# A new order of the first stage, and the second attention's blend in fp32r parts

## The reference

```python
weight = softmax(einsum('bct,bcs->bts', q * s, k * s))      # first attention, 512 x 512, over channels
h = einsum('bts,bcs->bct', weight, v)                        # 125 x 512
# second attention on layernorm(h): 8 heads of 64, 2 key/value heads, rope
scores = tanh((q2 @ k2.T) / 16 / 50) * 50
h = h + (softmax(scores) @ v2) @ Wo.T
# feed-forward on y = layernorm(h): a shared part for every token ...
out = (silu(y @ sw1) * (y @ sw3)) @ sw2
# ... and two of eight experts per token, by softmax(y @ gate_w) + expert_bias
out = out.at[token_idx].add(routed_out)
h = h + out
```

## Time and profile before

| | us |
|---|---|
| median of 3 runs | 5918.14 |
| the profiled execution's own time | 5922.86 |
| its span, first to last instruction | 5921.1 |
| TensorE busy, share of the span | 5784.0, 98% |
| VectorE busy | 4450.0, 75% |
| ScalarE busy | 3084.8, 52% |
| GpSimd busy | 2101.8, 35% |

### The profile page before, as it was taken

How to read it: one execution, slowest core, us unless ns; L and a number is a source line. 1 busy time by engine, 2 the same in 40 slices (tenths; PEclk the granted TensorE clock), 3 DMA queues, 4 the chain that set the end, 5 groups by cost and what they waited for, 6 DMA issues and landing times. The chain is left out here.

```text
span 5921.1 us, 109291 instructions
## 1 busy us (share of the span) xinstructions
PE 5784.0 (98%) x32259; PEld 5009.4 (85%) x32259; DVE 4450.0 (75%) x10104; ACT 3084.8 (52%) x5748; POOL 2101.8 (35%) x1711
## 2 busy tenths in 40 slices
PE   5999999999999999999999997899999999999999
PEld 4888888888888888888888886899999999999998
DVE  4888888888888888888888886666666766666665
ACT  3555555555555555555555553555555555555554
POOL 1333333333333333333333332333434444444343
PEclk8999999999999999999999999999999999999999
DMA  2111111111111111111111111777777777777762
GB/s 73 47 50 44 44 49 46 43 47 49 43 45 50 44 44 49 46 43 47 49 43 45 50 44 25 190 188 187 184 189 182 182 187 188 183 189 182 184 167 79
DMA packets 363663, 565.45 MB, mean 95 GB/s; under 512 B 92898, under 2 KB 187106, under 8 KB 363492
## 3 DMA queue, kind: packets, MB, share of 16 engines
q1 hardware_dynamic: 294276, 433.22, 24.2%
q0 software_dynamic: 69344, 131.70, 11.3%
HBM read 438.14 MB, written 138.42 MB: 97 GB/s over the span
## 5 line engine op out<-in xcount | busy, mean ns | idle before, releaser
L1438 POOL DMA_INDIRECT out_dram<-res,goal x273 | 560.8, 2054 | 1070.4 <-DMA entries<-routed_entries 480.8
L930 POOL TENSOR_SCALAR ve<-ag 125x1 f32<-125x1 f32 x256 | 56.1, 219 | 1618.3 <-DVE ag L755 942.2
L639 ACT ACTIVATE e<-ps,negmax 128x512 f32<-128x512 f32 x512 | 348.6, 685 | 513.5 <-PE ps L449 409.8
L1188 PE MATMUL ps<-rT_hi,up_hi 128*128 128x384 f32 x2548 | 552.3, 338 | 1.6 <-DVE rT_lo L1348 1.6
L1188 PE MATMUL ps<-rT_lo,up_hi 128*128 128x384 f32 x2548 | 552.1, 338 | 0.0
L1188 PE MATMUL ps<-rT_hi,up_lo 128*128 128x384 f32 x2548 | 552.0, 338 | 0.0
L1278 ACT ACTIVATE uT_hi<-egb 128x384 fp32r<-128x384 f32 x364 | 191.4, 526 | 572.3 <-DVE egb L1367 561.5
L1188 PEld LDWEIGHTS ps<-rT_hi,up_hi 128*128 128x128 f32 x2548 | 457.8, 188 | 9.8 <-issue 2.0
L1188 PEld LDWEIGHTS ps<-rT_lo,up_hi 128*128 128x128 f32 x2548 | 456.3, 188 | 0.0
L1188 PEld LDWEIGHTS ps<-rT_hi,up_lo 128*128 128x128 f32 x2548 | 456.2, 188 | 0.0
L942 POOL TENSOR_TENSOR qk_low<-X,qk_high 125x1024 fp32r<-125x1024 f32 x128 | 306.3, 2393 | 345.7 <-ACT qk_high L626 345.7
(11 more groups left out here) (220 smaller groups left out, 15549.2 us busy)
## 6 DMA issues: line engine op xcount, KB each, us to landing
raw<-in_L_ffn_w SPq DMA_DIRECT2D x182, 768.0 KB, 5.1
X<-in_x SPq DMA_DIRECT2D x128, 750.0 KB
raw<-in_L_ffn_w SPq DMA_DIRECT2D x91, 896.0 KB
raw<-in_L_ffn_w SPq DMA_DIRECT2D x273, 128.0 KB, 5.0
normed_rows<-y SPq DMA_DIRECT2D x128, 250.0 KB
out_dram<-h SPq DMA_DIRECT2D x128, 250.0 KB
rows<-normed_rows,entries POOLq DMA_INDIRECT x273
out_dram<-res,goal POOLq DMA_INDIRECT x273
```

The source lines that it names most:

```text
L639: nc.scalar.activation(e[:, i, :], ps[:, (i + 1) % 2, :], ACT.Exp, bias=negmax[:, i:i + 1], accum_out=total[:, i:i + 1]).then_inc(e_sb.sem, 1)
L1188: ins = nc.tensor.matmul(ps[:, bank, 0:GROUP], w[a][:, k, col:col + P], rT[b][:, k, :], start=(k == 0 and i == 0), stop=(k == KC - 1 and i ...
L1438: nc.gpsimd.indirect_dma_start(out, bass.IndirectOffsetOnAxis(ap=goal[group[1] % 2][:, i:i + 1], axis=0), res[i][:], None, bounds_check=la ...
```

## The change: what it does, and the diff

1. `attend` is done in fp32r parts. ScalarE rounds prob to `prob_cut[0]` (`soften_hi`), GpSimd makes `prob_cut[1] = prob - prob_cut[0]` (125 x 1000) . `vS` holds, per key/value head, the high values (64), a one, a zero, and the low values (64), so that one product of prob's high part with 130 columns gives both; prob's low part is multiplied by 66 columns. The fourth head of a bank has no room for 130 columns and uses 66 + 64 + 66. It makes 18 fp32r products per batch in place of 8 fp32 ones. `normalise` now adds the two halves: per key/value head two reciprocals, a multiply of 125 x 192, a multiply of 125 x 64, and three scalar_tensor_tensor of 125 x 64.
2. `attend` and `normalise` move one step later (lag 2), and so the shared feed-forward's second half (w3s, gate, choice, transposes of gb, down, ranks, placed) moves to lag 3. w1g of batch f is the last work of TensorE's step.
3. The normalising of e moves from VectorE to ScalarE (four Copies with a scale).
4. All five queues get a new order. On GpSimd it is: rstd 1, prob's low part, v's low part, the rope's add, rstd 2, the next q and k's low part, and the scatter last. On SyncE's queue the two output DMAs swap places.

The order of TensorE's step after: scores 0, 1 (t); w3s (g); scores 2, 3; transposes of v (t); of xn (a); `attend(0)`, `attend(1)` (f); q (a); transposes of gb (g); of attn (f); e 0, 1 (t); k/v (a); wo (f); e 2, 3 (t); down, all 11 (g); ranks (g); rope's transposes (a); blend high (t); transposes of y (f); second scores (a); blend low (t); w1g (f).

```diff
@@ TensorE @@
                     def attend(kv):
-                        pe.wait_ge(qkT_lo.sem, qkT_lo.at(a))
-                        pe.wait_ge(p_sb.sem, p_sb.at(a, kv + 1))
                         for j in range(G):
-                            last = nc.tensor.matmul(ps[0:C, 2 + kv, j * VW:(j + 1) * VW],
-                                                    prob[0:C, kv, j * C:(j + 1) * C],
-                                                    vaug[a[1] % 2][0:C, kv, :], start=True, stop=True)
+                            heads = slice(j * C, (j + 1) * C)
+                            wide = 2 * HD + 2 if j < APART else EW
+                            col = j * (2 * HD + 2)
+                            nc.tensor.matmul(ps[0:C, 7 - kv, col:col + wide], prob_cut[0][0:C, kv, heads],
+                                             vS[0:C, kv, 0:wide], start=True, stop=False)
+                            if j >= APART:
+                                nc.tensor.matmul(ps[0:C, 7 - kv, col:col + HD], prob_cut[0][0:C, kv, heads],
+                                                 vS[0:C, kv, EW:EW + HD], start=False, stop=False)
+                            last = nc.tensor.matmul(ps[0:C, 7 - kv, col:col + EW], prob_cut[1][0:C, kv, heads],
+                                                    vS[0:C, kv, 0:EW], start=False, stop=True)
                         last.then_inc(pv_ps.sem, 1)
...
+                    if has(2):
+                        pe.wait_ge(p_hi.sem, p_hi.at(f))
+                        pe.wait_ge(p_lo.sem, p_lo.at(f))
+                        pe.wait_ge(v_lo.sem, v_lo.at(f))
+                        pe.wait_ge(gb_sb.sem, gb_sb.at(g))
+                        attend(0)
+                        pe.wait_ge(ga_sb.sem, ga_sb.at(g))
+                        attend(1)
...
+                    if has(2):
+                        pe.wait_ge(attn_sb.sem, attn_sb.at(f))
+                        pe.wait_ge(xT_lo.sem, xT_lo.at(a))
+                        turn(3, attn[:, :, :].rearrange("p a b -> p (a b)")).then_inc(aT_ps.sem, 1)
@@ ScalarE @@
+                        for i in range(KC):
+                            nc.scalar.activation(e[:, i, :], e[:, i, :], ACT.Copy,
+                                                 scale=rz[:, i:i + 1]).then_inc(e_norm.sem, 1)
...
+                    def soften_hi(kv):
+                        act.wait_ge(p_sb.sem, p_sb.at(a, kv + 1))
+                        act.wait_ge(pv_ps.sem, pv_ps.at(f))
+                        nc.scalar.activation(prob_cut[0][0:C, kv, :], prob[0:C, kv, :], ACT.Copy).then_inc(p_hi.sem, 1)
@@ VectorE: order of the step after: bn 1 (a), nl (g), maxima 0, xn (a), ga, gb (g), maxima 1, chosen, m16 (g), xT_lo (a),
@@ 1/total (t), normalise 0, 1 (f), aT_lo (f), hT_lo (g), v_lo (a), e_lo 0, 1 (t), rope (a), h2, bn 2 (f), e_lo 2, 3 (t), y (f),
@@ h3 (g), qkT_lo (a), entries (g), yT_lo (f), placed (g)
+                    def normalise(kv):
+                        dve.wait_ge(pv_ps.sem, pv_ps.at(f, kv + 1))
...
+                        nc.vector.reciprocal(rd_v[:, 0:APART], both[:, :, HD])
+                        nc.vector.reciprocal(rd_v[:, APART:G],
+                                             flat[:, APART * wide + HD:APART * wide + HD + 1]).then_inc(rden_sb.sem, 1)
...
+                        nc.vector.tensor_tensor(ours[:, 0:APART, :], both[:, :, EW:wide],
+                                                rd_v[:, 0:APART, None].to_broadcast([C, APART, HD]),
+                                                ALU.mult).then_inc(both_sb.sem, 1)
+                        nc.vector.tensor_scalar(ours[:, APART, :], flat[:, APART * wide:APART * wide + HD],
+                                                rd_v[:, APART:G], None, ALU.mult)
+                        dve.wait_ge(both_sb.sem, both_sb.at(f, kv + 1))
+                        for j in range(APART):
+                            last = nc.vector.scalar_tensor_tensor(ours[:, j, :], both[:, j, 0:HD], rd_v[:, j:j + 1],
+                                                                  ours[:, j, :], ALU.mult, ALU.add)
+                        last.then_inc(attn_sb.sem, 1)
@@ GpSimd @@
                     if has(1):
                         rstd(a, ag1, ve1, rs1, ag1_sb, ve1_sb, rs1_sb, xn_sb)
                     if has(2):
+                        pool.wait_ge(p_hi.sem, p_hi.at(f))
+                        pool.wait_ge(pv_ps.sem, pv_ps.at(g))
+                        alone(pool)
+                        nc.gpsimd.tensor_tensor(out=prob_cut[1][0:C, :, :], in0=prob[0:C, :, :],
+                                                in1=prob_cut[0][0:C, :, :].bitcast(F32),
+                                                op=ALU.subtract).then_inc(p_lo.sem, 1)
...
                         rstd(f, ag2, ve2, rs2, ag2_sb, ve2_sb, rs2_sb, y_sb)
+                    if has(-1):
+                        cut_scores(back(t, -1))
                     if has(3):
                         pool.wait_ge(pick.sem, pick.at(g))
                         pool.wait_ge(place.sem, place.at(g))
```

More of the change, by code:

```diff
@@ L343, in alone, with product @@
             eng.sem_inc(past, 1)
-        def product(pe, dst, lhs, rhs, rows, c0, c1, lo, at, between=None):
+        def product(pe, dst, lhs, rhs, rows, c0, c1, lo, at):
             for i, (a, b) in enumerate(PASSES):
                 if i == 2:
-                    if between:
-                        between()
                     pe.wait_ge(lo, at)
@@ L397, in step @@
                         load(back(t, -1))
[L398 to L402, removed]
                     if has(2):
@@ L480, in step @@
                         scores(1)
-                    if has(2):
-                        pe.wait_ge(attn_sb.sem, attn_sb.at(f))
+                    if has(3):
                         pe.wait_ge(tanh_sb.sem, tanh_sb.at(f))
[L485 to L488, removed]
+                        product(pe, ps[0:C, 7, 0:HID], yT, w3s, P, 0, HID, yT_lo.sem, yT_lo.at(g)).then_inc(up_ps.sem, 1)
+                    if has(0):
+                        scores(2)
+                        scores(3)
                     if has(0):
                         pe.wait_ge(x_in.of(t), x_in.at(t))
-                        pe.wait_ge(attn_sb.sem, attn_sb.at(f))
+                        pe.wait_ge(qkT_lo.sem, qkT_lo.at(f))
                         for k in range(KC):
@@ L496, in step @@
                         last.then_inc(vT_ps.sem, 1)
-                    if has(3):
-                        down_part(2, 1)
-                        pe.wait_ge(hT_lo.sem, hT_lo.at(g))
-                        down_part(0, 0, c=1)
-                    if has(0):
-                        scores(2)
-                    if has(0):
-                        scores(3)
+                    if has(1):
+                        pe.wait_ge(xn_sb.sem, xn_sb.at(a))
+                        pe.wait_ge(place.sem, place.at(back(g, 1)))
+                        turn(3, xn).then_inc(xT_ps.sem, 1)
@@ new lines, in step @@
+                    if has(2):
[6 more added lines that the diff above has]
+                        attend(1)
+                    if has(1):
+                        pe.wait_ge(yT_lo.sem, yT_lo.at(g))
+                        pe.wait_ge(xT_hi.sem, xT_hi.at(a))
+                        product(pe, ps[0:C, 4, :], xT, wqkv, P, 0, D, xT_lo.sem, xT_lo.at(a)).then_inc(q_ps.sem, 1)
@@ L508, in step @@
                         product(pe, ps[0:C, 7, :], aT, woT, P, 0, D, aT_lo.sem, aT_lo.at(f)).then_inc(wo_ps.sem, 1)
[L509 to L539, removed]
-                        pe.wait_ge(h3_sb.sem, h3_sb.at(g))
-                        product(pe, ps[0:C, 6, 0:HG], yT, w1g, P, 0, HG, yT_lo.sem, yT_lo.at(f)).then_inc(up_ps.sem, 1)
                     if has(0):
@@ L692, in step @@
                         weights_hi(3)
-                    if has(-1):
-                        round_scores(back(t, -1))
                     if has(1):
@@ L792, in step @@
                     if has(1):
                         dve.wait_ge(xT_hi.sem, xT_hi.at(a))
[L794 to L800 removed]
+                        lo_part(xT, 3).then_inc(xT_lo.sem, 1)
@@ L974, in step @@
                         alone(pool)
-                        nc.gpsimd.tensor_tensor(out=qkr[0:C, :], in0=rc[0:C, :], in1=rsn[0:C, :],
+                        nc.gpsimd.tensor_tensor(out=rc[0:C, :], in0=rc[0:C, :], in1=rsn[0:C, :],
                                                 op=ALU.add).then_inc(rope_add.sem, 1)
+                    if has(2):
+                        rstd(f, ag2, ve2, rs2, ag2_sb, ve2_sb, rs2_sb, y_sb)
                     if has(-1):
                         cut_scores(back(t, -1))
+                    if has(3):
+                        pool.wait_ge(pick.sem, pick.at(g))
+                        pool.wait_ge(place.sem, place.at(g))
+                        alone(pool)
+                        for k in range(2):
+                            nc.gpsimd.indirect_dma_start(
```

(3 more changed lines are left out.)

442 lines of the change are left out of this document (226 added, 216 removed).

## The result

The changed kernel takes 6352.8 us (median of 4 runs, 6352.4 to 6353.6), the kernel before 5917.9 beside it: 1.073 times as long (95% interval 1.072 to 1.075). That is outside the range. It is rival B at both places, for which the prediction had worked out 6330.

A forecast was written before the change was run, and what follows sets the result against it. TensorE was taken as the bound. 128 steps x (0.88 for the blend - 0.45 for removed waits) = 55, plus 8 for the end: +63, 5986 against the profiled execution, 5981 as median. Range 5885 to 6200.

The forecast's parts named there:

- rival B: GpSimd subtractions hold VectorE's xn and y by the port lock: 6120 at one place (chance 0.15), 6330 at both (0.17).
- 1 us to spare: GpSimd: prob's low part, 2.34 us more, starts after rstd 1, done by 5.0; blend needs it about 6: cost 0.
- the likeliest case: The forecast itself: 5981 us, its own range 5950 to 6020, chance 0.32.
- a tie: Behind rstd 1, GpSimd's next instruction and VectorE's xn each start 0.03 us after the instruction ahead, so either may win.
- The blend's size: TensorE's blend: 16 records go (-1.69 us), 18 fp32r products come; +0.88 us a step taken.
- The lower end: Blend products cost as much as any narrow instruction, 18 x 0.106 = 1.91 us, so +0.22 a step.
- the upper end: Blend products cost the fp32 blend's price per column, 1.63 ns, 2.57 us in all, so +0.88 a step.
- The waits that the new order removes: TensorE: waits at the ranks (0.23), q (0.10) and last k/v products (0.12) go: -0.45 us a step, range 0.2 to 0.55.
- Normalising e, cost 0: ScalarE gets 3.7 us of copies a step beside TensorE's work; they end before attn's transposes, so cost 0.
- `normalise`: VectorE: 1.1 us per key/value head; at the upper blend price nothing waits, at the lower attn's transposes wait 0.2.
- The end: At lag 3 a chain from w3s to scatter runs once with nothing beside it: +8 us (0 to 12).
- rival A: TensorE: narrow blend products cost what a weight load costs, 0.106 each, with `normalise` in time: -21, 5897 us; chance 0.15.

The follow-up runs named there:

- the spare subtraction: Kernel before plus one unread 125 x 1000 GpSimd subtraction right behind rstd 1: 6124.2 us, ratio 1.034.
- the wait at y: Changed kernel, with GpSimd's subtraction for the next q and k waiting until y is written: 6290.7 us, ratio 1.062.
- the kernel without waits: Changed kernel with fp32 blend, old normalise, cut_scores after y, 1/total ahead of xT's low part, e's fourth row normalised on VectorE: 5854.5 us, ratio 0.989.
- the new order with the old blend: Changed kernel with fp32 attend, old normalise, no low parts of prob and v, and cut_scores waiting for y: 5954.2 us, ratio 1.006.
- the kernel with both waits: Changed kernel, with GpSimd's prob low part waiting until xn is written and cut_scores until y is written: 6064.7 us, ratio 1.024.
- that at xn: Changed kernel, with only prob's low part on GpSimd waiting until xn is written: 6152.4 us, ratio 1.039.
- prob's low part on VectorE: Changed kernel with cut_scores waiting for y and prob's low part moved from GpSimd to VectorE ahead of xn: 6105.4 us, ratio 1.031.
- the control: Kernel before plus one unread 125 x 1000 GpSimd subtraction behind v's low part: 5925.5 us, ratio 1.001.

## Why the prediction was wrong, point by point

**The step that failed** is "prob's low part ... Cost 0, with 1 us to spare, if nothing else is taken from GpSimd", and with it the choice of the likeliest case. The condition looked at GpSimd's time; what was taken was VectorE's: the hold at xn costs 200 to 226 us, and that of y, for which the sum had nothing either, 62 to 88. The mechanism stood in rival B with the right places and sizes (3.2 us a step foretold for the four waits, 3.1 measured), and the deciding question, who wins behind rs, was left at a tie because the two starts in the earlier trace rows are both 0.03 behind a recorded end. They weren't alike: the indirect DMA's successor there isn't a subtraction behind a pow. Whether VectorE or GpSimd wins, no row then at hand shows. The runs do: in the changed kernel, in each kernel that leaves one of the two places as it was, and in the kernel before with the spare subtraction, it is GpSimd in every step. `cut_scores` behind rstd 2 was weighed only in the rival; in the sum it had no term at all.

The "1 us to spare" wasn't there either. It stood on rstd 1 "done by 2.6", with the scatter ahead of it at cost 0. In the changed kernel it is done by 2.4, but there TensorE waits for y and the second scores and so gives GpSimd time. With the wait at y it is done by 3.5 to 3.6, with junk held ahead of the slots and the scatter; the low part would then end at 5.9 at the earliest, and the blend starts at 6.1 in the kernel without waits.

**The blend's size** was wrong, +0.88 for a measured 1.96 - 1.69 = +0.27 (0.29 against the 1.67 of the new order). The lower end, 18 x 0.106, was right, and the argument for the upper end ("the row nearest in kind") failed: 18 products of 64 to 130 columns cost 0.109 each on the mean, 16 records of 65 columns 0.106, so it is the count that is paid and not the columns. The page "TensorE: Matmul & The Clock Gate" of the Trainium skill ("LDWEIGHTS (loading the stationary operand)") gives a load its columns divided by 1.2 in nanoseconds, 104 ns for 125 as an estimate; the 0.109 here agrees.

**The waits that the new order removes** came out right. The rank stands right behind down:

```profile
1033.38 0.86 PE L432 MATMUL ps<-w2s_hi,hT_lo 128*125 128x512 f32 x3
1034.07 0.17 PE L563 MATMUL ps<-m,tri 125*125 125x8 bf16 x1
```

0.69 for three products of 512 columns, nothing lost. The kernel without waits has 27.39 against 27.93, -0.54 with the old blend (and with 1/total moved ahead and a fourth of e's normalising back on VectorE); 0.45 was foretold, 0.2 to 0.55 its range.

**Normalising e, cost 0,** was wrong where nothing else was late: 0.76 a step in the new order with the old blend. "e's copies end before attn's transposes" had left out that 1/total stands behind the choice of experts on VectorE.

**`normalise`** takes 1.28 per key/value head on VectorE's queue (1.1 foretold): its three steps of 64 columns are 0.19 apart, not 0.13. It is in time nevertheless where nothing ahead of it is late. By line and form, the kernel with both waits:

```profile
L473 PE MATMUL ps<-vS,prob_cut_hi 125*125 125x130 f32 x576 | 141.6, 303 | 57.2 <-issue 57.2
L422 PE MATMUL ps<-ident,attn 125*128 125x125 f32 x384 | 59.4, 277 | 2.4
```

attn's transposes wait 2.4 us in 96 steps, where the changed kernel has 70.0 in 89; the only other wait is the blend's for prob's low part. Without waits, at the clock's higher level, this kernel would need 27.39 + 0.29 = 27.68 a step, an estimate; with 57.2 / 97 + 0.16 = 0.75 that the blend loses on the mean that is 28.4, and 28.6 was measured. The rest, about 0.2, isn't explained.

**The end** grew by 16 and not by 8: from the last batch's first scores to the second stage's first product it is 137.7 us against 121.6. In the kernel without waits it is 124.9, so only about 3 are the longer chain.

**The sum by what was measured:** 27.39 (no waits, old blend) + 0.29 (parts) + 3.1 (the four waits) = 30.8 for the changed kernel's step; 30.88 is the mean of its 66 steps clear of the lower clock, 31.29 that of all, so the lower clock costs it 0.4 a step. Without the waits it would be 5854.5 + 128 x 0.29 = 5892 by estimate, close to rival A. No run shows this kernel: each place tried for prob's low part (behind rs, behind xn, on VectorE ahead of xn) makes something late. A place for `cut_scores` at which it meets neither y nor junk wasn't tried.

What lowered the clock stays open. Between 200 us and the last batch's first scores it was at the lower level for 99, 106, 20 and 328 us in the changed kernel, with both waits, with that at xn and with that at y. These falls lie 8 to 10 us into a step, behind a wait and the blend in parts, or 26 to 28, behind the waits for y and for the second scores. In the other kernels there was none, and three of them wait too: for attn (1.02 a step, prob's low part on VectorE), ahead of q (0.94, the spare subtraction behind rstd 1), for e (0.59, the old blend).

## What to carry to other kernels

Before a GpSimd instruction on SBUF is queued behind one that VectorE waits for, look at what VectorE does next: here a tensor_scalar from SBUF to SBUF, and an 8-column instruction with both sources in SBUF, waited out the whole GpSimd subtraction, and GpSimd's idle share says nothing against that. Such work goes where VectorE's next instructions read PSUM, as in the control. After a move, look at the small instructions that it now meets, and not only at the one that it left. And when a reordering brings less than it should, first list every TensorE wait with its releaser: the last two small edits here gave back 0.78 us a step, more than twice the 0.29 that the blend in parts costs.

## What was not expected

GpSimd starts its queued subtraction 0.02 to 0.03 before the recorded end of the power, and VectorE, which waits for that power, 0.03 to 0.14 behind it, so GpSimd's next instruction is first in every step recorded. The hold works from both sides: 2.35 us of GpSimd made xn 2.58, and 1.19 us of VectorE made a one-column GpSimd add 0.98. A hold that is taken from one place can turn up at another: junk went from 0.17 to 1.41 us when y went back to 0.55. And the bracket of a wait is about 0.16 less than the queue loses: 1.03 for 1.19, 0.71 for 0.87, 0.60 for 0.76.
